# A graph network's last layer over edge records packed by destination block, with sums in a moving window of PSUM

## The reference, cut to what matters

```python
# twelve layers (eight like this, four with tanh and no normalisation)
g = _l2_normalize(segment_sum(h[src] * edge_weight[:, None], dst))
h = _l2_normalize(jnp.concatenate([h, g], axis=1) @ W + b)
...
# the convolution
R = jax.nn.relu(abs_distances[:, None] @ w1 + b1) @ w2 + b2   # 448 numbers an edge
Y = spherical_harmonics(rel_vec)
Fj = features[src]
...  # msg: products of R, Y and Fj, 32 numbers an edge
out = out.at[dst].add(msg)
```

## Time and profile before

| | |
|---|---|
| median of 3 runs | 12853.25 us (12851.23 to 12859.91) |
| span of the profiled execution | 11187.8 us |
| its own time | not shown apart; the median stands for it, 1665.5 us more than the span |
| busy: TensorE, VectorE, ScalarE, GpSimd | 7977.6, 9110.1, 3152.1, 4719.6 us |
| mean granted TensorE clock | 0.804 of full speed |
| DMA | 1175.84 MB in 719340 packets, 105 GB/s over the span |

### The profile page before, as it was taken

The page is one execution under the profiler, slowest core; times in us unless marked ns, Lnnn a source line. Parts: engine busy times, 40 slices in busy tenths (PEclk is TensorE's granted clock), DMA queues, the critical chain, the costliest instruction groups (busy, mean ns, idle before and its releaser), DMA issues.

```text
span 11187.8 us, 339090 instructions
## 1 busy us (share of the span) xinstructions
PE 7977.6 (71%) x127894; PEld 5606.9 (50%) x127895; DVE 9110.1 (81%) x18642; ACT 3152.1 (28%) x7975; POOL 4719.6 (42%) x5783
## 2 busy tenths in 40 slices
PE   2555555400777877877877878786889988888994
PEld 2444444300666766766766767674444444444442
DVE  8777777658877877877877877778999999999995
ACT  0111111048222222222222222222444444444441
POOL 3777777610311311321221221232665656666661
PEclk9999999975988988988988988997665666566555
DMA  4111111147645655744745755662111111111111
GB/s 174 26 26 25 25 25 25 27 168 249 200 150 152 205 152 151 211 151 150 216 150 152 211 168 161 182 186 77 36 36 35 34 36 36 36 35 35 36 34 19
DMA packets 719340, 1175.84 MB, mean 105 GB/s; under 512 B 155346, under 2 KB 350241, under 8 KB 715001
## 3 DMA queue, kind: packets, MB, share of 16 engines
q1 hardware_dynamic: 435480, 1024.95, 28.9%
q0 software_dynamic: 146832, 67.20, 5.1%
q10 hardware_dynamic: 136012, 67.95, 2.4%
HBM read 1019.27 MB, written 140.22 MB: 104 GB/s over the span
## 4 chain that ended last, share of the span: by engine, by line
PE 41%; DVE 18%; issue 16%; ACT 3%; POOL 1%; DVEq 1%; DMA 1%; ACTq 0%; POOLq 0%; SPq 0%
PE psum L1959 10%; PE psum L1927 10%; PE psum L1942 6%; PE psum L2069 6%; PE psum L2050 3%; DVE space L1476 2%; DVE space L1475 2%; DVE space L1442 2%; PE psum L2034 2%; PE psum L2004 2%; DVE space L1480 2%; ACT space L1590 2%; DVE space L1487 1%; PE psum L2019 1%; ACT space L1595 1%
## 5 line engine op out<-in xcount | busy, mean ns | idle before, releaser
L714 POOL TENSOR_TENSOR claim_out<-claim_in 128x1 f32<-128x1 f32 x1199 | 309.9, 258 | 4943.4 <-DMA table<-space 2405.5
L789 POOL DMA_INDIRECT space<-feature_table,space x2000 | 1943.1, 972 | 612.0 <-issue 611.6
L2050 PE MATMUL psum<-w_mix,space 64*128 64x448 f32 x4144 | 1755.8, 942 | 0.0
L1622 ACT ACTIVATE space<-psum 128x375 f32<-128x375 f32 x2400 | 937.9, 435 | 2866.9 <-PE psum L1927 2862.6
L725 POOL DMA_INDIRECT slots<-space x1568 | 1507.0, 961 | 466.1 <-issue 412.8
L1141 DVE TENSOR_TENSOR space<-psum,space 128x320 f32<-128x320 f32 x2400 | 1065.7, 485 | 727.6 <-PE psum L1942 702.8
L1927 PE MATMUL psum<-space 128*32 128x125 fp8e4 x72000 | 1344.0, 223 | 227.5 <-issue 226.1
L1959 PE MATMUL psum<-space 128*128 128x96 bf16 x24000 | 1287.9, 206 | 217.8 <-issue 163.1
L1927 PEld LDWEIGHTS psum<-space 128*32 128x32 bf16 x72000 | 1077.4, 97 | 484.2 <-issue 474.0
L1959 PEld LDWEIGHTS psum<-space 128*128 128x128 fp8e4 x24000 | 1099.4, 96 | 375.6 <-issue 258.4
L1147 DVE TENSOR_TENSOR space<-space 128x320 f32<-128x320 f32 x2400 | 1059.5, 482 | 2.7 <-issue 2.7
(11 more groups left out here) (275 smaller groups left out, 11948.6 us busy)
## 6 DMA issues: line engine op xcount, KB each, us to landing
space<-marks SPq DMA_DIRECT2D x2400, 320.0 KB
marks<-space SPq DMA_DIRECT2D x100, 640.0 KB, 3.1
space<-distances ACTq DMA_DIRECT2D x200, 320.0 KB
space<-block_ids SPq DMA_DIRECT2D x198, 200.0 KB
slots<-space SPq DMA_DIRECT2D x82, 448.0 KB, 9.1
space<-feature_table,space POOLq DMA_INDIRECT x2072, 2.4
space<-src_rows SPq DMA_DIRECT2D x102, 320.0 KB, 4.0
slots<-space POOLq DMA_INDIRECT x1608, 2.1
```

What stands on the lines that cost most here:

```text
L789: g.indirect_dma_start(out=gathered_rows[:, half, t, :], out_offset=None, in_=feature_table, in_offset=bass.IndirectOffsetOnAxis(ap=row_in ...
L1622: a.activation(to[:, s0:s1, :, :], pair_picked[:, bank, 0:(s1 - s0) * PICK_COLS].rearrange("p (k c r) -> p k c r", k=s1 - s0, r=CAP), ACT.Copy
L2050: last = mm(radial[:, 2 * ring + odd, 0:MIX_S + MIX_V], hidden[odd * HIDDEN:(odd + 1) * HIDDEN, slot, upper * LANES:(upper + 1) * LANES], ...
```

## The change

The convolution no longer reads the 2000 slot tiles and the spilled list. All records of a destination block are packed one after another into a new DRAM tensor `dense`, in tiles of 128 records, with at least 4 tiles a block; the number of tiles depends on the edges.

- SP clears `dense` during the sort. VectorE computes from the pair counts where each run (up to 25 records of one pair of blocks) and each spilled half starts, the offset of each tile's sums, and the window of each turn (new steps between the slots read and the first marks).
- Before layer 0 GpSimd copies the spilled halves to `dense`. At the boundaries before layers 1 to 10 it copies ten source blocks' runs each (100 in all): SP loads a run of 100 destination blocks with five DMAs into one of two buffers (`load_runs`), GpSimd copies index and distances, writes records and distances with two indirect DMAs and waits for them to land (`scatter_run`), and that landing frees the buffer.
- The convolution goes over `dense` in turns of 40 tiles, as many as there are. A turn's tiles touch at most 11 blocks, so its sums go to a window of 352 columns in one of two PSUM banks. TensorE loads eight column offsets into registers ahead of each group's adds, and clears a window at the start of each turn; VectorE moves the sums of the turn before to `xs` after the first group of each turn.
- The spilled part, the chunks and `copy_index` are gone; the row numbers come by a DMA of 8-byte pieces (`load_index`), the records by one of 56-byte pieces.

The core of the diff:

```diff
+            def load_runs(layer):
+                first = RUNS_PER_LAYER * (layer - 1)
+                for k in range(RUNS_PER_LAYER):
...
+                    if not isinstance(layer, int) or k >= RUN_RING:
+                        sp.wait_ge(runs_scattered, 32 * (first + k - RUN_RING + 1))
+                    for j in range(CHUNKS):
+                        sp.dma_start(run_recs[j * UNIT_TILES:(j + 1) * UNIT_TILES, k % RUN_RING, :, :],
+                                     slot_tiles[lanes, bass.ds(steps[j], UNIT_TILES), :
+                                                ].rearrange("r t w -> t r w")).then_inc(run_loaded[k % RUN_RING], 16)
...
                 for q in range(RING):
                     load_marks(0, q)
+                if runs:
+                    load_runs(layer)
                 sp.wait_ge(h_ready, layer + 1)
...
+            def load_index(half, at):
+                sp.dma_start(index_words[:, half, :, :],
+                             dense_tiles[:, bass.ds(at, UNIT_TILES), 0:2]
+                             ).then_inc(index_loaded[half], 16)
...
+            def scatter_run(layer, k):
+                nth, slot = RUNS_PER_LAYER * (layer - 1) + k, k % RUN_RING
+                pool.wait_ge(run_loaded[slot], 16 * CHUNKS * (RUNS_PER_LAYER // RUN_RING) * (layer - 1)
+                             + 16 * CHUNKS * (k // RUN_RING + 1))
+                claim(16)
+                g.tensor_copy(run_index[0:BLOCKS, slot:slot + 1], run_row[:, bass.ds(nth, 1)])
+                g.tensor_copy(run_dist[0:BLOCKS, slot, :], run_recs[0:BLOCKS, slot, :, 2]).then_inc(dists_copied, 1)
+                pool.wait_ge(dists_copied, spilled_turns + nth + 1)
+                claim(14)
+                scatter_rows(run_recs[0:BLOCKS, slot, :, :].rearrange("p r w -> p (r w)"), run_dist[0:BLOCKS, slot, :],
+                             run_index[0:BLOCKS, slot:slot + 1], runs_scattered)
+                pool.wait_ge(runs_scattered, 32 * nth + 32)
+                claim(15)
...
+            def move_sums(i):
+                dve.load(window_regs, windows[0:1, bass.ds(2 * i, 2)])
...
+                v.tensor_tensor(xs_flat[:, bass.ds(to, WINDOW)], xs_flat[:, bass.ds(to, WINDOW)],
+                                conv_sums[:, bass.ds(bank, WINDOW)], ALU.add).then_inc(sums_moved, 1)
...
+            def add_group(i, g):
+                nth = i * PAIR_GROUPS + g
+                pe.load(half_regs[0:GROUP], tile_offsets[0:1, bass.ds(TURN_TILES * i + GROUP * g, GROUP)])
                 pe.wait_ge(lanes_marked, 2 * nth + 2)
                 pe.wait_ge(messages_ready, nth + 2)
                 for t in range(GROUP):
-                    tile = (g * GROUP + t) % UNIT_TILES
                     ring = ((2 * g + t // QUAD) % MARK_RING) * QUAD + t % QUAD
-                    to = (tile % SUM_BLOCKS) * D
-                    last = mm(conv_sums[:, tile // SUM_BLOCKS, to:to + D], lane_marks[:, ring, :],
+                    to = pe.snap(half_regs[t], min_val=0, max_val=BANK + WINDOW - D)
+                    last = mm(conv_sums[:, bass.ds(to, D)], lane_marks[:, ring, :],
                               edge_messages[:, BUFFER_OF[g] * GROUP + t, :], start=False, stop=True,
                               skip_group_check=True)
...
+            def clear_window(i):
+                pe.load(half_regs[0:2], windows[0:1, bass.ds(2 * i, 2)])
+                bank = pe.snap(half_regs[1], min_val=0, max_val=BANK)
+                pe.wait_ge(sums_moved, i + 1)
+                mm(conv_sums[:, bass.ds(bank, WINDOW)], zeros_bf[:, 0:LANES], zeros_bf[:, 0:WINDOW], start=True, stop=True)
```

More of the change, by code:

```diff
@@ L780, in _, with scatter_rows @@
                     gather_spilled(base + i, i, 16 * layer + 16, layer * UNITS)
+            def scatter_rows(recs, dists, rows, landed):
+                for to, data in ((dense, recs), (dense_dist, dists)):
+                    g.indirect_dma_start(out=to, out_offset=bass.IndirectOffsetOnAxis(ap=rows, axis=0), in_=data,
+                                         in_offset=None).then_inc(landed, 16)
+            def scatter_run(layer, k):
[11 more added lines that the diff above has]
+                claim(15)
@@ L782, in gather_unit @@
+            gather_layer(0)
+            with pool.Fori(1, 1 + RUN_LAYERS, 1) as layer:
+                for k in range(RUNS_PER_LAYER):
+                    scatter_run(layer, k)
+                gather_layer(layer)
+            with pool.Fori(1 + RUN_LAYERS, LAYERS, 1) as layer:
+                gather_layer(layer)
             def gather_unit(half, i):
                 pool.wait_ge(features_stored, 16)
-                pool.wait_ge(index_copied, 2 * i + half + 1)
+                pool.wait_ge(index_loaded[half], 16 * i + 16)
@@ new lines, in _, with conv_turn @@
+            TURN_STEPS = PAIR_GROUPS * 8
+            def conv_turn(i, first, last):
+                token = conv_step.enter(i, TURN_STEPS)
+                for g in range(PAIR_GROUPS):
+                    group_step(i, g, not last or g + 1 < PAIR_GROUPS)
+                    if g == 0 and not first:
+                        move_sums(i - 1)
+                if not last:
+                    conv_step.leave(token, 0)
+            framed_ready = project(0, 0)
+            summed = project_sums(0, framed_ready)
@@ new lines, in _ @@
+            apart = project_apart(0, summed)
+            conv_step.after(project_joint(0, apart))
+            turns = dve.value_load(conv_turns[0:1, 0:1], min_val=3, max_val=MAX_CONV_TURNS)
+            last = dve.value_load(conv_last[0:1, 0:1], min_val=2, max_val=MAX_CONV_TURNS - 1)
+            dve.wait_ge(tables_loaded, 16 * 3)
+            conv_turn(0, True, False)
+            with dve.Fori(1, last, 1) as i:
+                conv_turn(i, False, False)
+            conv_turn(last, False, True)
@@ L1557, in _ @@
+            move_sums(last)
+            dve.wait_ge(sums_moved, turns + 2)
             v.memset(waited[:, 0:1], 0.0).then_inc(x_updated, 1)
@@ L1761, in pair_step @@
                         load_far(i + 1, q8 // QUADS)
-            act.wait_ge(rec_cleared, 4)
-            for half in range(2):
-                copy_index(0, half)
+            act.wait_ge(runs_scattered, 32 * BLOCKS)
             for half in range(2):
@@ L1821, in _ @@
+            pair_step(last, True)
         @block.tensor
@@ L2119, in _ @@
[L2119 to L2134 removed]
+            pe.wait_ge(tables_loaded, 16 * 3)
```

580 lines of the change are left out of this document (276 added, 304 removed).

## The result

The changed kernel takes **11933.94 us** (median of 4 runs, 11912.0 to 11941.05), the kernel before 12852.24 us beside it: a ratio of 0.9278, 95% interval 0.9265 to 0.9291, 918 us less. The forecast was 12122 us with a range from 11980 to 12360.

The account below looks back on a forecast made before the run. No engine alone bounds the convolution; TensorE and VectorE hand work to each other. The terms, -590 - 236 + 31 + 30 + 12 + 13 + 4 + 5 = -731, take 12853 us to 12122 us, range 11980 to 12360.

Parts of the forecast that it names:

- The step that failed: Whole run: 1665.5 us of the measured time lie outside the profiled span of 11187.8 us and stay fixed.
- +4: Before the layers: two loads of 2560 pieces of 8 B ahead of the feature table, 2 us each, +4 us.
- Rival D: Whole run: more is won, since each stage may run slower than in the profiled execution; 12010 us, chance 0.08.
- Groups removed: Convolution: 250 main groups at 12.74 us become 205 at 12.66 us, -590 us.
- The tail: End of the convolution: 240.9 us of spilled groups go, some 5 us remain, -236 us.
- Register loads: Convolution, TensorE: eight offsets loaded ahead of each group's adds, 0.15 us for each of 205, +31 us; bounds 0 and 139.
- clear: Convolution, TensorE: two-register load and window clear at each turn's start, 0.73 us for each of 41 turns, +30 us.
- moves of sums: Convolution, VectorE: moving the previous turn's sums, mostly covered by waits, 0.3 us for each of 41 turns, +12 us.
- Planning and sort: Before the layers: VectorE's plan delays the first marks, +13 us; clearing the dense records in the sort, +5 us.
- The copies: Boundaries between layers: 100 run copies, 6.7 us a run, hidden behind the end of a layer, 0 us.
- B: Layer boundaries: costlier 56 B pieces make the run copies overflow, +234 us, 12360 us; chance 0.14.
- E: Layer boundaries: a run's five loads go to one engine each time, +1100 us, 13230 us, slower than before; chance 0.04.

Follow-up runs that it names:

- b_same3: The kernel before, unchanged, third repeat, which fell on chip 4, the slow chip: 12860.25 us.
- b_same: The kernel before, unchanged, run again for a second profile: 11186.22 us.
- a_same2: The changed kernel, unchanged, second repeat, on chip 4: 11899.95 us against 12851.1 and 12860.25 for the kernel before.
- a_18_tiles: The changed kernel with at least 18 tiles for each destination block instead of 4, so 230 groups instead of 205: 10799.65 us.
- b_same2: The kernel before, unchanged, second repeat: 11172.01 us.
- b_no_tail: The kernel before without the convolution's loops over the spilled turns: 10943.97 us against 11190.79.
- a_same: The changed kernel, unchanged, where the kernel before takes 11177.54 us: 10468.12 us, ratio 0.9362.
- a_load_twice: The changed kernel with the load of eight registers ahead of the adds done twice: 10466.02 us, ratio 0.9371 to the kernel before.
- a_runs20: The changed kernel with 20 runs copied at each of the first five boundaries instead of 10 at each of ten: 10591.7 us.
- a_no_runs: The changed kernel without the run copies between layers, so nearly all records are empty: 10750.53 us, ratio 0.9614 to the kernel before.

## Why the prediction was right, and where it failed

**The step that failed** is the first: "So 1665.5 us lie outside what the records show; I hold them fixed and work every term inside the span." Nothing lies outside. The profile of before was of an execution of 11190 us, the times beside it were of ones of 12850 us, and the difference is time inside the span, spread very unevenly over the stages. With the terms as they were, -731, the time came out at 12122; measured were -918. b_same3 against b_same: sort 1.25 times as long, the making of the marks and what lies around it (from the last L725 to the first L1984) 1.005, the layers 1.07, a group 16.02 / 12.67 = 1.264, the spilled part with the end (from the last main group) 279.2 / 261.1 = 1.07. Most of the gain is main groups, which are stretched most.

**The sum with the right factor.** The terms in the convolution are -590 - 236 + 31 + 30 + 12 = -753; times 1.264 that is -952. The rest (+13, +4, +5) stays: about -930, 11922 us. Measured are 11933.94. That it comes so near is in part luck. Stage by stage, b_same3 against a_same2: the layers start at 3318.6 in the one and 3319.3 in the other, the first group comes at 8585.9 and at 8561.2, and from there to the end it is 4272.7 us against 3337.1: -935.6, of a difference of 960.3. Against the profile after, whose layers start at 3349.9 and whose first group comes at 8624.9, it is 4272.7 against 3304.5: -968.2. Of this the end is 279.2 - 24.5 = 254.7, since it is stretched by 1.07 and not by 1.264, and the main groups are 681 and 714, where -590 + 31 + 30 + 12 = -517 times 1.264 are -654. On this chip the group costs 16.04 us before and 16.08 to 16.24 after, so less of the gain is given back by a longer group than elsewhere. The mechanism, most of the gain growing with the stretch of the groups, is shown; the single factor is only a rough one. a_same2's lines:

```profile
L2066 PE MATMUL psum<-zeros x12: 203/206/207, 3319.3 to 8078.9; 128*128 128x32 bf16 x12
L1636 DVE TENSOR_REDUCE space<-space x205: 1740/1747/1755, 8561.2 to 11873.8; 128x192 f32<-128x1536 f32 x103
```

**Rival D** was this, half thought through. It named the right mechanism ("each stage runs slower than in the profiled execution") but priced it with the mean of the whole run, 15%, and gave it 0.08. With the mean it gives 12010, still too high by 76. Its chance was too low as well: nothing in the profile spoke for a fixed 1.7 ms outside the records.

**Groups removed** (-590): right. 205 groups, as counted; the group of the changed kernel 12.87 to 12.92 us with its share of the turn's ends, forecast 12.9 to 13.1; each group's price shown by a_18_tiles.

**The tail** (-236): right, 247 measured by the times (221 to 285) and 236.5 by the traces.

**Register loads** (+31) and **clear** (+30), **moves of sums** (+12): near in sum, wrong one by one. From the first to the last of 250 main groups, four traces of the kernel before (the first profile, b_same, b_same2, b_no_tail) have 12.70 to 12.76 us a group with the four chunk ends in it; a_same, a_load_twice, a_18_tiles and a_runs20 have 12.87 to 12.92. Less 0.08 for the chunk ends the group grew by some 0.25 us (0.19 to 0.30), 50 us over 205, where 73 were forecast. But the load shows 0 to 17 us, and the clear none. The bound at nothing for the load was the right one: it lies in TensorE's wait for L1653. A term put at nothing is there instead: the adds with columns from registers start 0.1 us later, up to 20 us in all. It is not the durations of the matmuls, by which the prediction judged it (the earlier trace rows against the earlier trace rows); the adds still take 3.62 us. What makes up the rest of the 50 us was not taken apart, and no run tests the moves of sums. The load of two registers takes 0.547 us and not 0.37: the line drawn between 0.313 for one and 1.106 for sixteen does not hold, and eight take 0.591. The *Trainium skill* (DMA: Bandwidth & Descriptors, section Latency and other measured facts) has a floor of about 600 ns for such a load; the prediction set it aside by the row of the one-register load, 0.313 us, which stands against it; for two and for eight the page was nearer than the line.

**Planning and sort** (+13, +5): the layers start (first L2066) 18.6 us later in a_same than in b_same, 2831.0 against 2812.4. By L815,

```profile
L815 POOL DMA_INDIRECT slots<-space x1568: 955/962/1172, 172.8 to 2193.1; - x196
L2066 PE MATMUL psum<-zeros x12: 203/205/207, 2831.1 to 7339.3; 128*128 128x32 bf16 x12
```

the sort ends at 2193.1 instead of 2188.2; 13.7 are the planning. VectorE's first marks (L1280, L1092 before) start 13.0 us later against the end of the sort, as forecast. The 4.9 us of the sort are not shown: in b_same2, the kernel before, it ends at 2193.0 too.

**The copies** (0): right, and the issue window too (56 to 62 us at the ten boundaries of a_same, forecast 61). Rivals B and E are out: at 5.6 us a run (6.7 in the forecast) the pieces of 56 bytes are cheap and they do spread. The *Trainium skill* (DMA: Bandwidth & Descriptors, Specifications) has transfers below 512 B read, modified and written; the prediction made of it a factor of two on each piece and 8.3 us a run, and that price is not seen. Whether the pieces are so treated, no run here shows.

**What the prediction lacked**: from the first layer to the first group a_same takes 4980.1 us and b_same 4917.8, 62 us more, where +4 were forecast. It is in all traces at 11180 us: 4913.0 to 4939.1 us in four of the kernel before, 4970.5 to 5006.9 in seven of the changed one. a_no_runs shows the same without any copies (4978.8), so it is not their cost. On chip 4 it is not there (5267.3 before, 5275.0 and 5241.9 after). Of the 62 us, 9 are in the first eight layers, 33 in the units of the last four (from a layer's first matmul to its last add 326.6 us instead of 318.4), 7 in the step into the convolution (144.3 us from the last add of a unit to the first L1636, 137.2 before) and 14 in the boundaries of the last four. Twelve of these go with the clock. The same step between two layers takes 68.6 or 80.5 us in b_same, by the clock that is granted:

```profile
6419.70:6488.30 68.60, 41.99 (x601) 37.65 (x598) 51.19 (x69) 17.41 (x36) 0.00 (x0) 0.63 0.11 42
6809.50:6890.00 80.50, 54.58 (x599) 50.23 (x597) 51.37 (x69) 18.06 (x36) 0.00 (x0) 0.52 0.10 36
```

and a_same has one more of the long kind. What lengthens the units of the last four layers stays open; the clock granted in them is 0.97 to 0.99 in both kernels.

## What to carry to other kernels

Lay the profiled execution's span beside the measured time first. Where they differ by more than some microseconds, don't hold the difference fixed: in every execution here it was time inside the stages, and each term of the sum has to be worked out with the stretch of its own stage, as one of the likely cases and not as a remote one. Where the stretch is not shown, take one that lies wholly in the changed stage as the end of the range: 753 us out of the 3.42 ms of the convolution, with all 1665 us in that stage, are 1120 us, and a low end of about 11750; with the 1665 us spread over the sort and the convolution they are 976, and 11900.

A wait that stands between two engines' hand-overs is a place to put small work for nothing: a load of registers of 0.6 us ahead of the adds, even twice, did not move the time. A column that comes from a register may cost something where the same matmuls' durations show nothing: compare when they start. And where an experiment takes data away, look whether the addresses have become equal: the gathers of nearly equal rows here landed in 13.2 us instead of 2.4.

## What the runs showed of the hardware

- One chip of five ran the same program 15% slower with instructions of the same duration, within 4% in the rows above. The extra time is in pauses of TensorE, or in its signals arriving late, at fixed places of its program: in the changed kernel after the third and the fourth group of nearly every turn (in the profile after on average 18.9 and 20.4 us from one L1636 to the next instead of 13), in the kernel before after the third and the fifth (18.3 and 21.0 in b_same3).
- It is not TensorE's clock that makes the difference: the granted clock of the whole run was 0.807 in the 11929.4 us span of the changed kernel and 0.807 in the 11153.1 us span of b_same, and on chip 4 once 0.725 (b_same3) and once 0.828 (a_same2). The sort takes 2519 us at 0.70 in b_same3 and 2536 at 1.00 in the profile after. The stages of b_same3:

```profile
0.00:2696.00 2696.00, 1095.69 (x7863) 851.59 (x7864) 1733.22 (x4210) 235.87 (x590) 1551.47 (x1781) 0.70 0.13 36
3318.00:8586.00 5268.00, 4162.97 (x109432) 3454.72 (x109432) 3907.20 (x8525) 1174.64 (x2939) 1060.74 (x1790) 0.88 0.52 160
8586.00:12560.00 3974.00, 3007.26 (x9897) 1360.91 (x9897) 2910.99 (x4957) 1297.37 (x3319) 1940.76 (x2085) 0.58 0.14 28
```

- In the slow executions the trace lacks semaphore events. b_same has 34912 of them up to the end of the sort, 66223 from the first layer to the first group and 44965 from there to the end; b_same3 has 12346, 66927 and 14030. They are missing in the two stages that are 1.25 times as long, and not in the layers, which are 1.07 times as long. The *Trainium skill* (NOTIFIC — the notification-queue block, section Overflow: three behaviours, one of which stalls the engine) says that a queue of such records, when full, drops new ones, overwrites the oldest or holds up the engine that makes them. Lost records and a held engine would fit the two observations, though as two different settings of a queue. But TensorE makes most of its records in the layers (109430 matmuls in 4.9 ms against 10479 in 3.4 ms from the first group on), where the stretch is least. No run here tells the cause; it stays open.
- Gathers that nearly all read one row loaded GpSimd's queue 22.0% instead of 5.2% with fewer bytes and landed in 13.2 us instead of 2.4; VectorE waited up to 11.5 us for the record load beside them.
